# A two-layer transformer on one core: layer 1's turned scores and exps follow its maxima by six heads instead of eight

## The reference

```python
# layer 0 (x: 4 x 512 x 256; attention_bias: 4 x 16 x 512 x 512)
x = _ln(src) * (1.0 + scale) + shift                     # scale, shift from the time step
scores = einsum('bhqd,bhkd->bhqk', q / 4, k) + attention_bias
probs = softmax(where(src_mask, -inf, scores))
x = x + (ctx @ Wo + bo)
h = _ln(x) * g2 + beta2
out0 = x + _gelu2(h @ W1 + b1) @ W2 + b2                 # x * sigmoid(1.702 x)
# layer 1
h = layernorm(x, gamma1, beta1)
attn = softmax(where(causal, einsum('bhqd,bhkd->bhqk', Q, K) / 4, -inf))
x1 = x + (attn @ V) @ Wo + bo
x2 = x1 + gelu(layernorm(x1, gamma2, beta2) @ W1 + b1, exact) @ W2 + b2
return x + gate_score * (x2 - x)
```

## Time and profile before

| | us |
|---|---|
| median of 3 runs (1034.28 to 1042.74) | 1039.39 |
| the profiled execution | 1040.08 |
| its span in the trace | 1038.4 |
| TensorE busy in the span | 847.4 (82%) |
| VectorE busy | 611.7 (59%) |
| ScalarE busy | 499.6 (48%) |
| POOL busy | 417.2 (40%) |

### The profile page before, as it was taken

One profiled execution on the slowest core, in us unless ns is written; L12 is line 12 of the kernel. 1 busy time (PEld: TensorE's weight loads), 2 busy tenths in 40 slices (PEclk: granted clock), 3 DMA queues, 4 the chain that ended last, 5 costly groups with the idle time before them and its releaser, 6 DMA issues.

```text
span 1038.4 us, 14648 instructions
## 1 busy us (share of the span) xinstructions
PE 847.4 (82%) x4830; PEld 475.3 (46%) x4830; DVE 611.7 (59%) x1693; ACT 499.6 (48%) x879; POOL 417.2 (40%) x422
## 2 busy tenths in 40 slices
PE   3578988899956777898998876899999895699778
PEld 1244445447522333465545433455546362446245
DVE  6798775774738824657847834656836743536121
ACT  1156776766701365566732455566742344044421
POOL 3846368854302129386401228395501122022320
PEclk8779989999986998999998998999999997889869
DMA  8796889434590049356791049356651118400000
GB/s 259 89 220 203 160 288 221 134 116 137 155 131 1 1 55 150 102 173 191 134 184 42 2 95 151 111 173 192 125 71 42 42 49 134 41 1 2 21 1 21
DMA packets 84154, 114.70 MB, mean 110 GB/s; under 512 B 9800, under 2 KB 49516, under 8 KB 84080
## 3 DMA queue, kind: packets, MB, share of 16 engines
q1 hardware_dynamic: 84080, 113.77, 48.5%
HBM read 86.28 MB, written 2.10 MB: 85 GB/s over the span
## 4 chain that ended last, share of the span: by engine, by line
PE 60%; DVE 17%; issue 7%; ACT 6%; DMA 5%; SPq 3%; POOL 2%; DVEq 0%; ACTq 0%; POOLq 0%
PE psD L897 11%; PE psD L909 10%; PE psE L929 8%; PE psC L942 5%; PE psD L869 4%; PE psS L921 4%; PE psC L973 4%; PE psS L951 3%; DMA k<-work 3%; PE psD L885 3%; DVE tiles L1333 3%; SPq L401 3%; PE psE L961 2%; DVE junk L1348 2%; PE psD L855 2%
## 5 line engine op out<-in xcount | busy, mean ns | idle before, releaser
L546 POOL TENSOR_TENSOR tiles<-tiles,mask_neg 128x512 f32<-128x512 f32 x240 | 282.0, 1203 | 103.8 <-DMA tiles<-in_fside_Bx16xSxS 85.3
L1333 DVE CUSTOM_DVE_ANT_0 tiles<-psS,tiles 128x512 f32<-128x512 f32 x256 | 174.2, 688 | 152.9 <-PE psS L921 128.8
L670 ACT ACTIVATE prob<-psE 128x512 f32<-128x512 f32 x256 | 151.4, 594 | 118.2 <-PE psE L929 110.7
L1348 DVE CUSTOM_DVE_ANT_0 junk<-psS,later 128x128 bf16<-128x128 f32 (+3 forms) x256 | 121.2, 489 | 138.1 <-PE psS L951 137.5
L661 ACT ACTIVATE tiles<-tiles,rmax 128x512 f32<-128x512 f32 x224 | 161.0, 720 | 68.0 <-DVE rmax L1333 67.3
L929 PE MATMUL psE<-ident,tiles 128*128 128x128 f32 x1024 | 166.3, 287 | 3.4 <-ACT prob L670 3.1
L929 PEld LDWEIGHTS psE<-ident,tiles 128*128 128x128 f32 x1024 | 121.9, 145 | 81.7 <-issue 36.7
L682 ACT ACTIVATE prob<-psE 128x512 f32<-128x512 f32 (+1 forms) x192 | 95.8, 526 | 117.8 <-PE psE L961 116.6
L897 PE MATMUL psD<-hT,w 128*128 128x512 f32 x256 | 131.9, 626 | 18.4 <-DVE work L1274 14.7
L585 POOL TENSOR_SCALAR_AFFINE_SELECT prob<-prob 128x256 f32<-128x256 f32 x128 | 52.9, 437 | 221.6 <-ACT prob L682 221.6
L909 PE MATMUL psD<-w,work 128*128 128x256 f32 x512 | 135.2, 386 | 5.4 <-ACT hT L713 4.8
(11 more groups left out here) (112 smaller groups left out, 943.8 us busy)
## 6 DMA issues: line engine op xcount, KB each, us to landing
tiles<-in_fside_Bx16xSxS SPq DMA_DIRECT2D x256, 256.0 KB, 2.9
q<-work SPq DMA_DIRECT2D x96, 128.0 KB, 5.6
k<-work SPq DMA_DIRECT2D x96, 128.0 KB, 8.1
w<-in_L_cond_W SPq DMA_DIRECT2D x12, 1024.0 KB, 5.9
res<-in_x SPq DMA_DIRECT2D x4, 512.0 KB, 8.5
out<-x SPq DMA_DIRECT2D x4, 512.0 KB, 5.0
mask_u<-in_mask_Bx1xSxS_bk SPq DMA_DIRECT2D x4, 256.0 KB, 8.2
q<-mT SPq DMA_DIRECT2D x48, 4.0 KB, 1.7
```

Of the source, the lines that this page charges most:

```text
L546: pool.tensor_tensor(tile(b, s), tile(b, s), mask_neg[:, tile_of(s)[1], :], ALU.add).then_inc(masked_p, 1)
L670: act.activation(prob0[:, part_no % 2, j, :, s % 2 * P:(s % 2 + 1) * P], psE[:, e_no(0, b, s) % 2, :].rearrange("p (k q) -> p k q", k=T), ...
L1333: dve.tensor_tensor_reduce(tile(b, s), psS[:, n % 2, :], tile(b, s), 1.0, -3e38, ALU.add, ALU.max, rmax[0][:, s:s + 1]).then_inc(s_drained, 1)
L1348: dve.tensor_tensor_reduce(junk[:, n % 2, 0:w], psS[:, n % 2, 0:w], later[:, S - w:S], 1.0, -3e38, ALU.add, ALU.max, rmax[1][:, h * T + t: ...
```

## The change

`LAG` becomes 6. So Y phases have 88 slots instead of 96: a head and a tail of six steps, and ten steps with both. ScalarE's `keep_channels` moves to the slot in which TensorE runs `turn_channels`, one earlier than the formula had it, because at `LAG` 6 the turn of group 3's maxima comes in the next slot and needs the same PSUM bank. The numbers in `PLANS` stay.

```diff
-LAG = 8
+LAG = 6
 Y_SLOTS = 4 * (H + LAG)
...
-                    if slot == 4 * (LAG + 2 * G + 3):
+                    if slot == 4 * (LAG + 2 * G + 3) - 1:
                         keep_channels(1, b, 0)
```

## The result

The changed kernel takes **1061.53 us** (median of 4 runs, 1059.55 to 1061.79), the kernel before 1039.91 in the runs beside it (4 runs, 1034.28 to 1042.74). The ratio is **1.0212, 95% interval 1.0171 to 1.0252**: 21.6 to 22.0 us slower, where 22.3 was forecast. The profiled execution took 1061.7 us, its span 1059.7.

What follows compares the result with a forecast made beforehand. TensorE, busy 847 of 1038 us, bounds the kernel, but Y0 to Y2 hand on by role copies. Y0 1.5 + Y1 3.8 + Y2 7.0 + Y3 10 = 22.3 us: 1062 against 1039.4, range 1051 to 1070.

Steps and rivals of the forecast that it cites:

- Y3's loads: Y3 from slot 24: ten new table loads start head 2's exps +10.1 us later than head 0's before, two heads included.
- the two heads: Steps 6 and 7: two more heads of turned scores, about 2.1 us of matmuls, contained in Y3's +10.1.
- The rival by which the loads are hidden: Y3: ScalarE's own pace doesn't count, so Y3 gets +1.1 and the kernel takes 1053 us; chance 0.06.
- the rival of a dearer switch: Y3: a table switch costs more than its load, +10 us, kernel 1072, or 1076 with the skill's drain; chance 0.05.
- One reading of the prediction: Y3, steps 6 and 7: eight inner products, the scores and all else filled 9.7 us, so one takes under 2.4.
- The rest of Y3: Y3 besides the loads: tail, moved values, row waits and channels' copy −1.0, slower clock +1.
- The waits for rows: Y phases: rows land 3.8 to 3.9 us after the turn; group 3 waits 1.9 in Y0, Y2, Y3, 1.1 in Y1.
- tied to the copies: Y0 to Y2 hand on a fixed time after step 17's turn or Y2's QK products: +1.5, +3.8, +7.0 us.
- the rival of a hand-over not tied to step 17: Y0 to Y2: role copies land sooner, phases hand on at their own ends; kernel 1051 us; chance 0.14.
- the turn of group 3: Y0: this turn moves by +2.4 us and the role copies follow; POOL's masks hide a part, leaving +1.5.
- The values of a group: Values of one group move to step 14: +2.4 us of TensorE at full clock; Y0's step 16 without them −2.8.
- The other side: Rival that the shorter phase wins: −3.5 us from Y3, nothing from phases tied to copies, kernel 1036; chance 0.06.

Runs made afterwards that it cites:

- experiment 1: Tanh in place of Gelu in Y3's feed-forward, on the changed kernel: 1.0109, median 1048.37 us; the same edit on the kernel before: 1.0002.
- experiment 2: Changed kernel with Y3's eight inner products due in slots 20 to 22, ahead of the first exp: 1.0182, median 1056.60 us.
- the control of experiment 1: Kernel before (eight heads of lag) with Tanh in place of Gelu in Y3's feed-forward: 1.0002.
- e6_roles8: Kernel before with one chunk's 12 role copies issued ahead of the rows of group 3's maxima in Y0 and Y1: 1.0081.
- e8_y012: Kernel before with lag 6 in Y0, Y1 and Y2 and lag 8 kept in Y3: 1.0086, median 1047.57 us.
- e14_masks: Kernel before; Y1's first role copies right behind group 3's rows, POOL's six next-X masks ahead of set_x1 in Y0 and Y1: 0.9956, median 1033.41 us.
- e3_roles: Changed kernel with one chunk's 12 role copies issued ahead of the rows of group 3's maxima in Y0 and Y1: 1.0193.
- e5_y3only: Kernel before with lag 6 in Y3 alone and lag 8 in Y0, Y1 and Y2: 1.0119.
- e10_mix: Lag 6 in Y0 and Y1, 8 in Y2 and Y3, turn two slots earlier, first role copies ahead of group 3's rows; against the kernel before: 1.0036.
- Experiment 5: Changed kernel with the turn of the maxima and ScalarE's copy of them two slots earlier: 1.0184, median 1056.67 us.
- experiment 6: One chunk's 12 role copies ahead of group 3's rows in Y0 and Y1: 1.0193 on the changed kernel, 1.0081 on the kernel before.

## Why the prediction was right

**The total and its make-up.** 22.3 us were forecast, 22.0 measured. The two spans differ by 21.3, with +1.1 ahead of Y0 and -3.8 behind Y3 that the change can't have made. Without these two it is some 24. By the experiments Y3 costs 12.4 us and the other phases 8.9, where 10 and 12.3 were forecast. So the mechanisms were right, and the hit within 0.3 us is luck: too little for Y3 and somewhat too much, as far as the medians tell, for the rest.

**Y3's loads: right in mechanism, near in size.** The exps of head 2 start 22.0 us behind slot 24 (931.4 to 953.38), where those of head 0 started 11.7 behind it (919.9 to 931.59): +10.3, forecast +10.1. In this term 2.1 us were for the two heads and so 8.0 for the loads; experiment 1 gives the loads 10.0 us by the traces and 10.9 by medians. The two heads by themselves cost less than was put for them: in the two kernels with Tanh the same exps start 11.4 and 10.3 us behind slot 24, which is 1.1 and not 2.1. The rival by which the loads are hidden falls by it. So does the rival of a dearer switch: in the alternating stretch the next instruction starts 0.01 to 0.02 us behind the load, ahead of Gelus as ahead of exps. The 1.97 us that this rival rested on are TensorE's: in the control of experiment 1 no load stands ahead of the first of these activations, and it still comes 3.27 us behind the copies after T2, no sooner than with the load. The drain that the Trainium skill adds to each switch ("ScalarE: Activation LUTs", "What ACT_TABLE_LOAD costs") would have made ten of them, by an estimate from its figure, 13.8 us dearer; no switch of the stretch shows it.

One reading of the prediction was wrong and did no harm: the 9.7 us of steps 6 and 7 held five inner products (21 matmuls of L897), not eight. In experiment 2, where nothing else runs, a product takes 1.8 us, still less than the 2.4 that the argument needs.

**The rest of Y3: put at 0, and more than 3.** From slot 24 to the end of Y3 it is 60.0 to 60.1 us in four traces with lag 8 (the kernel before, e6_roles8, e8_y012, e14_masks) and 73.5 to 73.7 in three with lag 6 (the changed kernel, e3_roles, e5_y3only); a fifth trace with lag 8, e10_mix's, has 64.3, at a granted clock of 0.87 behind the first exps against 0.96 in the kernel before. Leaving that one aside it is +13.6 us, of which 10.3 are the stretch with the loads and **3.3 lie behind it**, where the prediction had -1.0 for the tail and +1 for the clock. Of these 3.3 the new wait of 2.66 us for VectorE's division, before 0.58, is 2.1, and the rows' wait, 2.5 instead of 1.9, 0.6; the rest is not taken apart. With Tanh in both kernels these 3.3 are 2.6, so they are mostly not the loads'. That in the pair of the table Y3 is only 11.6 longer comes from ahead of slot 24, which was reached 36.4 us into the phase instead of 38.4, over the same work, at a granted clock of 0.79 against 0.77; in all the traces with the inner products at their old slots this takes 36.0 to 39.7 us, with either lag.

**The waits for rows: the total right, the places not.** Adding the prediction's entries gives 4 x 1.9 + 1.1 + 1.0 + 0.2 = 9.9 us; 9.9 were measured, in six waits. Groups 3 of Y0, Y2 and Y3 have 2.78, 2.78 and 2.52, since the turned scores that stand behind the turn are only the three or four pieces of head 11 (0.6 to 0.8 us of TensorE, then idle). Group 2 of Y0 has 0.91 and that of Y3 0.49, group 0 of Y1 0.41, and group 3 of Y1, put at 1.1, has none. That the sum agrees is luck. Experiment 5 adds what the prediction did not weigh: this wait has VectorE's read-out of psM right behind it.

**Y0 to Y2: tied to the copies.** +2.1, +4.7 and +5.6 in the pair, +1.4, +2.9 and +6.8 by the means of several traces, against 1.5, 3.8 and 7.0. The step on which it rests, a fixed distance from the first role copy to the next phase's first scores, held to 1.2 us in all three. For Y1 and Y2 the rival of a hand-over not tied to step 17 falls by the traces: TensorE's waits for the copies grew to 10.76 and 12.21 us. For Y0 the two traces don't tell, since the wait there isn't put down to a copy and the phase's own end came 3.0 us later too (95.2 us instead of 92.2, where it was said to hardly move), but in experiment 6 X1 started at once when the copies went first. Only Y1's end came early, by 2.3 us; Y2's came 1.7 us later. By medians the three phases cost 8.9 us (4.7 to 13.1), not surely less than 12.3.

Inside Y0 the turn of group 3 stood 76.8 us behind the phase's start and stands at 81.3: +4.5, where I had put +2.4. Of it 3.9 arise between the turns of groups 2 and 3 (12.1 us before, 16.0 after). The channels' work, now ahead of the turn, is 2.0 of these (0.85 of wait, 0.63 of matmuls, 0.47 of wait for the copy; the prediction put +0.4), and the wait for group 2's rows 0.9. The values of a group are 0.5: 4.50 us at 370.04, where the kernel before has 4.01 at 370.37 in the same stretch. Both ran near half clock (granted 0.51 and 0.58); the prediction had the group that comes at full clock, +2.4, against -2.8 for step 16 without its group. X1's first scores came 4.1 us later in the cycle, and by Y1's start 2.1 were left, since X1 was 2.0 us shorter (128.1 and 126.1 us); whether POOL's masks did that, as forecast, or the clock, stays open.

**The other side.** The shorter tail was to be worth 3.5 us at most where nothing is tied. Waits for exps did shrink from 18.2 to 10.0 us, but the rows' waits and the longer hand-overs took that up, and the loads came on top. No run with lag 6 or 7 in any phase was surely faster than the kernel before.

## What to carry to other kernels

Before a stage is slid along another, list which functions ScalarE computes in the slots where they will overlap: two that need different tables make every alternation a load. Where no other engine needs longer, ScalarE's queue of activations plus loads is then the length of the stretch. A phase whose successor waits for a chain of copies hands on by these copies' start, so a shorter tail buys nothing until that start moves. SyncE's queue is in order, so look at what the copies overtake when they move: ahead of the rows of group 3 they lost more than they won, behind these and ahead of the weights and the store, moved together with the masks, they won. When a wait is removed, look for the one that ends just behind it (here copies and masks): moving both, the copies behind the rows, won 0.4%; moving the copies alone, ahead of the rows, lost 0.8%.

## What the runs showed that I had not expected

The stretch behind Y3, which no edit touches, has two lengths: 54.6 to 55.2 us in eight traces, with a granted clock of 0.75 to 0.86 in its first 20 us, and 57.9 to 58.5 in six, with 0.66 to 0.71. Each is found with lag 6 and with lag 8. From slot 24 of Y3 to its end, on the other hand, the traces of one order agree within 0.2 us, with one exception (e10_mix, lag 8, 64.3 us instead of 60.0 to 60.1), so that is the place to read Y3's cost from. Tanh and Exp share a table and Gelu and Exp don't: 7 loads in the program against 19. The same 32 matmuls of a group's values took 2.36 us in Y1 before and at 980.18 after, but 4.01 in Y0 before and 4.50 in Y0 after, at granted clocks of 0.58 and 0.51: a price at full clock fits only some of their places, in either kernel.
